# Mamba mixer of a decoder layer: the cross term joins the skip term on GpSimd, and two of the third-tap steps move between the two weighings on VectorE

## The reference

```python
zxBCdt = x @ in_proj_w.T
z, xc, Bp, Cm, dtm = split(zxBCdt)        # 512, 512, 8, 64, 64 columns
dt = softplus(Bp + dt_bias)               # one step size for each of 8 heads
xc = silu(depthwise_causal_conv(xc, conv_w, conv_b))     # 4 taps along time
xh = xc.reshape(B, L, 8, 64)
a_bar = exp(dt * -exp(A_log))
# scan over time: h = a_bar * h + Cm (outer) xh ;  y_t = h . dtm
y = y + xh * D_param                      # the skip term
y = y * silu(z)
y = rms_norm(y, norm_w) @ out_proj_w.T
x = layernorm(x + y)
```

## Time and profile before

| what | us |
|---|---|
| median of 3 runs | 2431.78 (2431.63 to 2433.71) |
| the profiled execution | 2424.99 |
| its span | 2423.2 |
| busy in the span: PE / DVE / ACT / POOL | 2191.4 / 1790.1 / 1396.7 / 1258.2 |
| one steady round of the mixer | 23.43 |

### The profile page before, as it was taken

One profiled execution on the slowest core, in us unless ns is written; L12 is line 12 of the kernel. 1 busy time (PEld: TensorE's weight loads), 2 busy tenths in 40 slices (PEclk: granted clock), 3 DMA queues, 4 the chain that ended last, 5 costly groups with the idle time before them and its releaser, 6 DMA issues. The chain is left out here.

```text
span 2423.2 us, 53605 instructions
## 1 busy us (share of the span) xinstructions
PE 2191.4 (90%) x15804; PEld 1910.5 (79%) x15805; DVE 1790.1 (74%) x4428; ACT 1396.7 (58%) x3046; POOL 1258.2 (52%) x1411
## 2 busy tenths in 40 slices
PE   6999999999997897999999999999958999999776
PEld 5777777777775786888888888888848999999733
DVE  7888888888886424676777777677746777777778
ACT  5565565655653424666666666666626665556533
POOL 4677676776765001343434344343435776667755
PEclk9999999999998898999999999999979999999955
DMA  4011011110100453222222222222246877777588
GB/s 146 27 31 39 26 39 35 30 39 26 39 30 22 164 201 101 80 93 84 94 77 82 91 78 82 79 95 77 75 156 203 254 242 220 242 226 238 174 291 269
DMA packets 185263, 278.49 MB, mean 115 GB/s; under 512 B 26076, under 2 KB 107492, under 8 KB 185188
## 3 DMA queue, kind: packets, MB, share of 16 engines
q1 hardware_dynamic: 171140, 240.84, 31.8%
q0 software_dynamic: 12960, 35.67, 4.1%
q10 hardware_dynamic: 1088, 1.07, 0.1%
HBM read 184.13 MB, written 93.38 MB: 115 GB/s over the span
## 5 line engine op out<-in xcount | busy, mean ns | idle before, releaser
L1439 ACT ACTIVATE b_wk_f<-b_ps_s,b_nmx 128x77 f32<-128x77 f32 x1024 | 234.6, 347 | 15.4 <-DVE b_nmx L1487 15.4
L570 DVE SCALAR_TENSOR_TENSOR a_conv<-a_xc_pad,a_cw,a_conv 128x256 f32<-128x256 f32 x384 | 237.2, 677 | 8.4 <-ACT a_conv L457 8.4
L1447 ACT ACTIVATE b_pT<-b_ps_pT 77x1024 f32<-77x1024 f32 x128 | 130.7, 1021 | 142.3 <-PE b_ps_pT L1345 142.3
L2054 POOL DMA_INDIRECT made_scratch<-c_o_s,c_to x142 | 147.8, 1041 | 86.4 <-issue 42.4
L112 PE MATMUL c_ps_h<-c_xT_hi,c_w 128*128 128x256 f32 x568 | 168.0, 296 | 26.6 <-DMA c_b_c<-in_c_b 20.6
L1926 ACT ACTIVATE c_hid<-c_ps_h,c_b_c 128x256 f32<-128x256 f32 x284 | 111.6, 476 | 134.4 <-issue 76.0
L1503 DVE TENSOR_TENSOR b_oT_lo<-b_ps_oT,b_oT_hi 128x512 fp32r<-128x512 f32 x128 | 88.0, 687 | 130.6 <-ACT b_oT_hi L1453 130.6
L1732 POOL CAST w<-b_w_raw 128x256 f32 (+1 forms) x32 | 13.6, 425 | 323.9 <-DMA b_w_raw<-in_c_w 323.9
L1430 ACT ACTIVATE b_qT<-b_ps_q,b_bq_s 128x256 f32<-128x256 f32 x256 | 107.7, 473 | 112.4 <-PE b_ps_q L114 109.6
L1970 DVE TENSOR_TENSOR c_h_lo<-c_hid,c_h_hi 128x1024 fp32r<-128x1024 f32 x71 | 97.5, 1373 | 91.5 <-ACT c_h_hi L1935 60.9
L112 PE MATMUL c_ps_o<-w,c_h_hi 128*128 x568 | 160.0, 282 | 3.5 <-DVE c_h_lo L1970 3.5
(11 more groups left out here) (271 smaller groups left out, 7858.8 us busy)
## 6 DMA issues: line engine op xcount, KB each, us to landing
c_w<-parts_scratch SPq DMA_DIRECT2D x71, 1024.0 KB
c_xa<-sent_scratch SPq DMA_DIRECT2D x71, 260.0 KB, 2.9
d_got<-made_scratch SPq DMA_DIRECT2D x32, 512.0 KB, 5.4
keys_scratch<-k_k_s SPq DMA_DIRECT2D x8, 1232.0 KB, 4.8
b_kz<-keys_scratch SPq DMA_DIRECT2D x64, 154.0 KB, 2.8
b_vv<-values_scratch SPq DMA_DIRECT2D x32, 308.0 KB
a_xT_f<-in_xT SPq DMA_DIRECT2D x32, 256.0 KB, 3.1
a_x_f<-in_x SPq DMA_DIRECT2D x32, 256.0 KB, 2.7
```

What stands on the lines that cost most here:

```text
L570: dve.scalar_tensor_tensor(out=conv[:, m, :], in0=xc_pad[:, m, k:k + L], scalar=cw[:, m, k:k + 1], in1=conv[:, m, :], op0=ALU.mult, op1=AL ...
L1439: last = act.activation(pe_[:, u.par, c, :], s_scores[:, c // (C // GM), c % (C // GM), :], ACT.Exp, bias=nmx[:, u.par, c:c + 1])
L1447: act.activation(pT[:, u.par, :, :], ps_pT[0:LK, :, :], ACT.Copy).then_inc(s_pTc, 1)
L2054: pool.indirect_dma_start(routing.made, bass.IndirectOffsetOnAxis(to[:, t.slot, c:c + 1], 0), o_s[:, t.par, c, :], None).then_inc(s_sent[t ...
```

## The change

GpSimd's skip term for chunk 1 goes to a new buffer `x1d`; when VectorE has the scaled cross term `off_r` ready, GpSimd adds the two into `xd[:, 1]`, and the one addition on VectorE (L675) takes in both. The addition into `t2` in `join` goes away, and y of chunk 1 is made from `t1` directly. For that the cross term has to be ready sooner: on TensorE `out` is cut into two halves, and `mix_off` goes between them, ahead of `mix`. On VectorE `off_r` becomes a step of its own, `scale_off`; two of the four third taps go between `weigh(0)` and `weigh(1)`, the other two behind `scale_off`; `add_d` goes ahead of `normalise`.

```diff
@@ -184,7 +184,7 @@
         rc = sb("rc", [P, 2 * H])
         t1 = sb("t1", [P, NT, DI])
         off_r = sb("off_r", [P, DI])
-        t2 = sb("t2", [P, DI])
+        x1d = sb("x1d", [P, DI])
         y = sb("y", [P, 2, NT, DI])
         sq = sb("sq", [P, DI])
         ss = sb("ss", [P, 2, NT])
@@ -235,8 +235,8 @@
             sem(n) for n in ("xhi", "conv", "ylo", "zs", "v", "na", "gm", "mt", "sx", "sp", "l", "res", "st",
                              "mv", "x1", "t1", "or"))
 
-        s_xlo, s_cx, s_xd, s_lm, s_t2, s_y, s_ri, s_ve, s_rs = (
-            sem(n) for n in ("xlo", "cx", "xd", "lm", "t2", "y", "ri", "ve", "rs"))
+        s_xlo, s_cx, s_xd, s_lm, s_x1d, s_y, s_ri, s_ve, s_rs = (
+            sem(n) for n in ("xlo", "cx", "xd", "lm", "x1d", "y", "ri", "ve", "rs"))
 
         N_LOADS = 8
 
@@ -418,23 +418,25 @@
                         last = pe.transpose(ps_yT[:, m, P * c:P * c + P], y[:, b.par, c, P * m:P * m + P], ident)
                 last.then_inc(s_yT, 1)
 
-            def out(b):
-                if b.before(1):
-                    pe.wait_ge(s_wout, MI + 2)
-                pe.wait_ge(s_ylo, b.count(1, 1))
-                if b.known() and b.value() >= n_seq - 2:
-                    pe.wait_ge(s_res, b.ago(1).count(NT, NT))
-                else:
-                    pe.wait_ge(s_bcc, b.ago(-2).count(1, 1))
-                for c in range(NT):
+            def out(c):
+                def run(b):
+                    if c == 0:
+                        if b.before(1):
+                            pe.wait_ge(s_wout, MI + 2)
+                        pe.wait_ge(s_ylo, b.count(1, 1))
+                        if b.known() and b.value() >= n_seq - 2:
+                            pe.wait_ge(s_res, b.ago(1).count(NT, NT))
+                        else:
+                            pe.wait_ge(s_bcc, b.ago(-2).count(1, 1))
                     for m in range(MI):
                         last = split3(pe, ps_out[:, c, :], pair(yT_hi, yT_lo, slice(None), m, slice(P * c, P * c + P)),
                                       pair(wo_hi, wo_lo, slice(None), m), m == 0, m == MI - 1)
-                last.then_inc(s_out, 1)
+                    last.then_inc(s_out, 1)
+                return run
 
             run_steps(pe, n_seq, [
                 (in_x, 0), (turn_y, 2), (in_z, 0), (in_bc, 0), (step_size, 0), (scores, 1), (decay(0), 1), (turn_x, 1),
-                (decay(1), 1), (out, 2), (mix, 1), (mix_off, 1)])
+                (decay(1), 1), (out(0), 2), (mix_off, 1), (out(1), 2), (mix, 1)])
 
         @block.scalar
         def _(act):
@@ -479,7 +481,7 @@
             def y_high(b):
                 act.wait_ge(s_yT, b.count(1, 1))
                 if not b.before(1):
-                    act.wait_ge(s_out, b.ago(1).count(1, 1))
+                    act.wait_ge(s_out, b.ago(1).count(NT, NT))
                 act.activation(yT_hi[:, :, :], ps_yT, ACT.Copy).then_inc(s_yhi, 1)
 
             def take_bc(b):
@@ -512,7 +514,7 @@
                 act.wait_ge(s_T, b.count(1, 1))
                 if not b.before(1):
                     act.wait_ge(s_Y, b.ago(1).count(NT, NT))
-                    act.wait_ge(s_xd, b.ago(1).count(1, 1))
+                    act.wait_ge(s_xd, b.ago(1).count(NT, 1))
                     act.wait_ge(s_cx, b.ago(1).count(1, 1))
                 act.activation(x_t[:, :, :], p45[:, :, :], ACT.Copy).then_inc(s_xt, 1)
 
@@ -558,13 +560,13 @@
                     dve.wait_ge(s_bc, b.ago(2).count(1, 1))
                 dve.tensor_copy(xT_hi[:, b.par, :, :], xT_f[:, b.par, :, :]).then_inc(s_xhi, 1)
 
-            def taps(first, end):
+            def taps(first, end, blocks=range(MI)):
                 def run(b):
 
                     if first == 0:
                         dve.wait_ge(s_tap, b.count(1, 1))
                     for k in range(first, end):
-                        for m in range(MI):
+                        for m in blocks:
                             if k:
                                 dve.wait_ge(s_conv, b.count(12, 4 * (k - 1) + m + 1))
                             dve.scalar_tensor_tensor(out=conv[:, m, :], in0=xc_pad[:, m, k:k + L],
@@ -641,7 +643,7 @@
 
             def residual(b):
 
-                dve.wait_ge(s_out, b.count(1, 1))
+                dve.wait_ge(s_out, b.count(NT, NT))
                 dve.wait_ge(s_ri, b.count(2, 2))
                 dve.wait_ge(s_x_in[b.par], b.half * 16 + 16)
                 if not b.before(1):
@@ -667,16 +669,18 @@
 
             def add_d(b):
 
-                dve.wait_ge(s_xd, b.count(1, 1))
-                for c in range(NT):
+                for c in range(NT):
+                    dve.wait_ge(s_xd, b.count(NT, c + 1))
                     dve.wait_ge(s_Y, b.count(NT, c + 1))
                     if not b.before(1):
                         dve.wait_ge(s_y, b.ago(1).count(NT, NT))
                     dve.tensor_tensor(t1[:, c, :], p01[:, c, :], xd[:, c, :], ALU.add).then_inc(s_t1, 1)
+
+            def scale_off(b):
                 dve.wait_ge(s_off, b.count(1, 1))
                 dve.wait_ge(s_rc, b.count(1, 1))
                 if not b.before(1):
-                    dve.wait_ge(s_t2, b.ago(1).count(1, 1))
+                    dve.wait_ge(s_xd, b.ago(1).count(NT, NT))
                 dve.tensor_tensor(off_r[:, :].rearrange("p (h d) -> p h d", h=H),
                                   p7[:, :].rearrange("p (h d) -> p h d", h=H),
                                   rc[:, 0:H].unsqueeze(2).to_broadcast([P, H, HD]), ALU.mult).then_inc(s_or, 1)
@@ -700,7 +704,8 @@
 
             run_steps(dve, n_seq, [
                 (prep_once, 0), (x_high_next, 0), (taps(0, 1), 0), (y_low, 2), (gate, 0), (bias_dt, 0), (mask_g, 1),
-                (taps(1, 2), 0), (weigh(0), 1), (weigh(1), 1), (taps(2, 3), 0), (normalise, 3), (add_d, 1),
+                (taps(1, 2), 0), (weigh(0), 1), (taps(2, 3, (0, 1)), 0), (weigh(1), 1), (scale_off, 1),
+                (taps(2, 3, (2, 3)), 0), (add_d, 1), (normalise, 3),
                 (silu_conv, 0), (log_decay, 0), (residual, 2)], spare=2)
 
         @block.gpsimd
@@ -723,11 +728,15 @@
                                    rc[:, H:2 * H].unsqueeze(2).to_broadcast([P, H, HD]), ALU.mult).then_inc(s_cx, 1)
                 if not b.before(1):
                     pool.wait_ge(s_t1, b.ago(1).count(NT, NT))
-                for c in range(NT):
-                    last = pool.tensor_tensor(xd[:, c, :].rearrange("p (h d) -> p h d", h=H),
-                                              x_t[:, c, :].rearrange("p (h d) -> p h d", h=H),
-                                              d_b[:, :].unsqueeze(2).to_broadcast([P, H, HD]), ALU.mult)
-                last.then_inc(s_xd, 1)
+                pool.tensor_tensor(x1d[:, :].rearrange("p (h d) -> p h d", h=H),
+                                   x_t[:, 1, :].rearrange("p (h d) -> p h d", h=H),
+                                   d_b[:, :].unsqueeze(2).to_broadcast([P, H, HD]), ALU.mult).then_inc(s_x1d, 1)
+                pool.tensor_tensor(xd[:, 0, :].rearrange("p (h d) -> p h d", h=H),
+                                   x_t[:, 0, :].rearrange("p (h d) -> p h d", h=H),
+                                   d_b[:, :].unsqueeze(2).to_broadcast([P, H, HD]), ALU.mult).then_inc(s_xd, 1)
+                pool.wait_ge(s_x1d, b.count(1, 1))
+                pool.wait_ge(s_or, b.count(1, 1))
+                pool.tensor_tensor(xd[:, 1, :], x1d[:, :], off_r[:, :], ALU.add).then_inc(s_xd, 1)
 
             def spread_l(b):
 
@@ -748,12 +757,8 @@
                     pool.wait_ge(s_sq, b.ago(2).count(NT, NT))
                 pool.wait_ge(s_zs, b.count(1, 1))
                 pool.tensor_tensor(y[:, b.par, 0, :], t1[:, 0, :], zs[:, b.par, 0, :], ALU.mult).then_inc(s_y, 1)
-                pool.wait_ge(s_or, b.count(1, 1))
-                if not b.before(1):
-                    pool.wait_ge(s_y, b.ago(1).count(NT, NT))
-                pool.tensor_tensor(t2[:, :], t1[:, 1, :], off_r[:, :], ALU.add).then_inc(s_t2, 1)
-                pool.wait_ge(s_t2, b.count(1, 1))
-                pool.tensor_tensor(y[:, b.par, 1, :], t2[:, :], zs[:, b.par, 1, :], ALU.mult).then_inc(s_y, 1)
+                pool.wait_ge(s_t1, b.count(NT, NT))
+                pool.tensor_tensor(y[:, b.par, 1, :], t1[:, 1, :], zs[:, b.par, 1, :], ALU.mult).then_inc(s_y, 1)
 
             def inv_rms(b):
 
```

## The result

The changed kernel takes 2499.64 us (median; 2495.16 to 2501.05) against 2431.91 for the kernel before on the same chip: ratio 1.0274, 95% interval 1.0256 to 1.0292. It is 2.7% slower. The forecast was 2427.2 in a range of 2409 to 2448.

The account below looks back on a forecast made before the run. No engine was full; a cycle of waits, TensorE's 1.6 us for GpSimd's second y, set the pace. Steady rounds +7.8 and -9.0, mixer's end -3.4: sum -4.6, profiled 2420.4, median 2427.2, range 2409 to 2448.

Parts of the forecast that it names:

- Rival 2: VectorE's second `lm` beats the cast in every round, so all are long: +15, 2447, slower; chance 0.14.
- rival 3: TensorE's longer wait before `decay(0)` lowers its clock, `exp_decay` comes later: +17, 2444, slower; chance 0.06.
- A to L: VectorE's part of a round from the first L675's start to L638's start: 4.74 forecast, 5.03 before.
- Rival 4: Blocks overlap better than counted and TensorE becomes the bound, round 21.9: 2382; chance 0.05.
- L-4.03: A time in us relative to the start of L638 on VectorE, the mark L of a round.
- a margin of 0.06: On VectorE the cast issues at L+2.04, ahead of the second `lm` at L+2.10, in rounds without a loop branch.
- the two lengths: VectorE from L638's start to L585's start: 5.58 without a loop branch, 6.79 behind one.
- long rounds: The 12 steady rounds behind the two-round loop's branch, where the second `lm` beats the cast: 24.08 each, +7.8 together.
- Y to A: VectorE's part of a round from L585's start to the first L675's start: 12.55 forecast, 11.80 before.
- short rounds: The 16 steady rounds without a loop branch, where the cast beats the second `lm`: 22.87 each, -9.0 together.
- L to Y: VectorE's part of a round from L638's start to L585's start: 5.58 or 6.79 forecast, 6.60 before.
- Just in time: ScalarE, from `in_x` through L477, finishes at A+11.4 against VectorE's gate at A+11.45.

## Why the prediction was wrong

**The loss in the forecast's own terms.** Rival 2 (all rounds long) was +15 and rival 3 (the clock) +17 on 12 rounds. Both came, and for all 28 rounds: +15, 28 x 1.4 = +39, and A to L at 5.20 instead of 4.74, 28 x 0.46 = +13. Sum +67, measured +67.7 by the medians and +70.2 by the profiled executions. That it comes so near is partly luck: the +13 is a measured term and not a forecast one, and the first rounds cost 3.1 that the forecast didn't have. The -3.4 in rival 2 for the mixer's end was right in size (3.0). Rival 4's 2382 is a slip, its own sum gives 2386; nothing hangs on it.

**The step that failed first in the chain: the moved `normalise`.** The forecast priced L665 against GpSimd's products and stopped there. It didn't follow what the step releases: the store at the head of SP's queue, the load of `in_xT` queued behind it, 3.0 us of landing, the cast. The load left at L-4.03 before and leaves at L-0.28 now; 335.32 and 2.9 to 3.0 are 338.2 to 338.3, where the cast starts. That is L+2.64, behind the second `lm`, in every round. The forecast took the cast's time from VectorE's own order (L+2.04 or L+2.37) and gave rival 2 a chance of 0.14 for a margin of 0.06; it came true for another reason. With the load first, the two lengths are exactly 5.62 and 6.80 against 5.58 and 6.79, in alternating rounds.

**The second, and the larger: the clock at 0.06.** The mechanism was named, with its place and price: a first product after such a wait at 1.2 GHz, `decay(0)` at 3.64 instead of 1.96, 1.4 a round. It was applied only to the long rounds, and the chance was far too low for a wait that the forecast itself put at 2.3 in 12 rounds of 28. Measured: mostly 3.75 after a wait of 2.31, 1.95 when fillers leave 0.33, Y to A 13.99 against 12.58. In the changed kernel every round has the 2.3, since every round is long. But the clock didn't need the first failure: with the load first, where the forecast's two lengths of L to Y are there, Y to A is 14.1 in the mean and the short rounds have the slow `decay(0)` after a wait of 1.16. So even with L to Y as forecast the 1.4 would have come in nearly all rounds, up to +39 and not +17; that kernel takes 2480.35.

**The third: ScalarE.** "Just in time" rested on `in_x`, the only wait that the earlier trace rows show. L628 is the other one: ScalarE overwrites `conv`, which L628 reads, and the reordering put L628 behind `normalise`. The list of waits of after has it in 20 rounds with up to 3.2. That is ScalarE's idle time and not its cost; with three fillers and the load first it reaches VectorE's gate with 9.5 us in 13 rounds, and what it cost in the changed kernel wasn't isolated.

**The fourth: what the tail was worth.** The forecast's first paragraph put TensorE's 1.6 down to a tail made of the cross term, L680, L754 and L756. With the cross term and its scaling early and the addition left in the tail, 1.5 of the 1.6 stayed. With the addition out of it too (two fillers, the load and silu first) at most 0.5 is left, and still the round isn't shorter than before: other waits took its place. The second L675's product was taken to be ready at A+0.64; L677 starts at A+1.42 in the changed kernel, A+1.73 with only the cross term early and A+1.15 in one of the filled rounds, mostly because TensorE's mixing product (L403) for that chunk isn't there: the row with 1.73 names it, and the list of waits of after does in 13 rounds. In the other two rows the 0.74 and 0.48 ahead of it are put down to "issue", so for them it is inferred. A to L is 4.83 to 5.20 for that, not 4.74. So of the gain that the forecast saw in the tail nothing is left to measure: with the clock held, the load early and silu first the round is 23.86 against 23.44 before.

**What held.** The waits before `turn_y` and for L754 are gone; `lm` starts 0.25 after L640 (335.85 against 335.60). The two taps between the weighings take 2.45, forecast 2.44 (from Y+5.79 to Y+8.23); second weighing 2.06, ending at Y+10.23 where the clock is undisturbed, forecast 10.20; Y to A 12.58, forecast 12.55. The addition in `xd` took 1.39, forecast 1.15 behind a block. L717 goes ahead of the fourth tap in long rounds. The Trainium skill (SBUF — State Buffer, Who interferes with whom) has a second engine fully blocked for the whole of the first's instruction. The trace agrees: a chain of six such blocks, worked out to end at Y+10.20, ends at Y+10.23.

## What to carry over

Before pricing a moved step on its own engine, list what it releases elsewhere: a store at the head of an in-order queue held up the load behind it, and issuing that load first gave back 19 of the 68 us. Putting the one moved step, `normalise`, back gave 46. Where an edit moves TensorE's wait to another place and makes it longer, look at the granted clock first, and price it for every round and not only for those with the longest wait. And test whether the wait that a change removes is set by the step it removes: taking the product and its scaling out of the tail, with the addition left in, kept 1.5 of 1.6.

## What was not expected of the hardware

The clock holds at 1.00 with one wait of 1.56 a round and doesn't with one of 2.31 (0.87 to 0.92). With waits of 2.31 and 1.16 in turn, the products after the shorter one are as slow as after the longer (3.75 and 3.62). And it is not whole with waits of up to 1.4 before `decay(0)` (0.93 to 0.98) in the kernel with `normalise` first, which also stands 8.3 us in 21 rounds before L418 (up to 0.6) and 8.3 in 13 before `in_x` (up to 1.1). So the wait just before the slow products doesn't decide alone. What does wasn't settled. Work whose result nobody reads paid for itself there: some 2 us of products a round made the changed kernel 43.6 us faster.
